# A decoder kernel on one core: every fourth product with B made by GpSimd instead of VectorE

## The chip, the cores and the metric

The kernel runs on one core of a Trainium2 chip. What counts is the device time of one execution, in microseconds (us), the median of several. The engines are named as in the profile: PE is TensorE, DVE is VectorE, ACT is ScalarE, POOL is GpSimd, SP is the queue that issues most of the DMAs.

## What is computed

A decoder over an input x of 8 batches x 256 rows x 256 channels, all in float32. First comes a stack of four layers (causal linear attention with 16 heads, then a feed-forward part), then a cosine-similarity term with a context and a small gated pair of experts, then a selective state-space mixer, a cross attention, and a mixture of eight experts with a capacity. The change touches the state-space mixer only:

```
dA = exp(einsum('bld,dn->bldn', dt, A))                 # b, l=256, d=512, n=16
u  = einsum('bld,bln->bldn', x, Bc) * dt[..., None]     # the product with B
decay = clip(floor(dA * 2**15), 0, 32767) / 2**15
h[t] = decay[t] * h[t-1] + u[t]                         # along l, for each (d, n)
y  = einsum('bldn,bln->bld', h, Cc) + x * D
```

## The kernel before

All engines run hand-written instruction streams that meet in semaphores. A batch pair (2 batches, W = 512 rows) is the unit of the outer loops; there are four pairs, p = 0 to 3. In the mixer stage the channels d lie on the partitions in four blocks of 128 (c = 0 to 3), and the 16 states n are taken two at a time (NG = 2), in eight groups g. That gives 32 units a pair, unit i being group g = i // 4 and channel block c = i % 4, so 128 units in all. Every unit works on tiles of 128 x 1024 float32 (2 states x 512 rows).

For unit i:

- ACT makes the decay: an exponential (line 921, two halves), a rounding to int16 steps (line 932) and the way back to float (line 937), into one of three buffers `dA`.
- `drive(i)` (lines 1538 to 1545) on DVE multiplies `dtx` (dt times x, channel block c) by the rows of B, and writes `uh[i % 3]`. Both inputs lie in SBUF. It waits for the rows of B (`rows_in`) and, from the fourth unit on, for `ysum_done` of unit i - 3, which used the same buffer.
- `unit(i)` (lines 1547 to 1563) on DVE: the scan along the rows (line 1555, in place in `uh`), a slice of the cross attention of the pair before (`cross(i - 1)`), `drive(i + 1)`, a slice of the next pair's first part (`head(i)`), and the product with the rows of C (line 1563, in place, both inputs in SBUF).
- `state_sum(i)` on PE (lines 2072 to 2077) adds the two states of the unit into a PSUM bank by a product with the identity (line 2076) and then raises `ysum_done`.

`mixer(p, q, n)` is called on each engine for the overlapped work of three pairs: the units of pair p, the cross attention of pair q = p - 1 and the first part ("head") of pair n = p + 1. The calls with units are (0, -, 1), (1, 0, 2), (2, 1, 3) and (3, 2, -). So the units of pair 0 have no cross slices beside them, and the units of pair 3 have no head slices.

Of POOL little is asked here. In the mixer it computes 1/sqrt(variance) for the layer norms by `deviations` (a 128 x 4 addition at line 580, a 128 x 4 power at line 581): three times a pair for the head, whose statistics DVE makes in units 0, 8 and 21 and whose results it wants in units 1, 9 and 22 (line 1426). At the end of a pair it sets the start columns of `dA` to zero (line 691). In the layer stack POOL adds bias rows (line 611, 128 x 512, and line 616, 128 x 1024) and copies rows (line 598).

Of the kernel before, what the change touches and what calls it, by code (L numbers as in the profile page):

```python
# [9 lines left out]
ALU = mybir.AluOpType  # L10
# [3 lines left out]
P = 128  # L14
# [5 lines left out]
TT = 4  # L20
W = TT * P
# [8 lines left out]
IC = DI // P  # L30
NG = 2
UNITS = NS // NG * IC
# [16 lines left out]
HEAD_STEPS, TAIL_STEPS, CROSS_STEPS = 45, 5, 6  # L49
ACT_STEPS = 2 * UNITS  # L50
CROSS_SLOTS = 38
ROUTED_EARLY = 36
VALUE_COPIES = (0, 1, 6, 8)
LAST_SLOTS = (9, 12, 15, 18, 21, 24, 27, 30)
# [77 lines left out]
def hold(eng, sem, value):  # L132

    eng.wait_ge(sem, value)
    eng.sem_inc(HELD[0], 1)
# [21 lines left out]
def ssm_and_cross(eng, body):  # L157

    body(None, None, 0)
    body(0, None, 1)
    with eng.Fori(0, PAIRS - 2) as r:
        body(r + 1, r, r + 2)
    body(PAIRS - 1, PAIRS - 2, None)
    body(None, PAIRS - 1, None)


def begun(p, q):  # L170


    if p is not None:
        return p + 1, p, 0 if q is None else q
    return (0, 0, 0) if q is None else (PAIRS, PAIRS, q)
# [27 lines left out]
def decoder(nc, t, out):  # L203
    ctx = ExitStack()

    def sem(name):
        return ctx.enter_context(nc.semaphore(name))
# [82 lines left out]
    zs, xs, dt, dtx = a(IC, W), a(IC, W), a(IC, W), a(IC, W)  # L290
# [5 lines left out]
    Bs, Cs = zip(*((a(NG, W), a(NG, W)) for _ in range(2)))  # L296
    units_at = a.at
    dA, uh = [a(NG, W) for _ in range(2)], [a(NG, W) for _ in range(2)]
# [55 lines left out]
    def cross_banks(p, n):  # L354
# [40 lines left out]
    rows_in, starts_ready = [sem(f"rows_in{j}") for j in range(2)], sem("starts_ready")  # L395
    da_ready, scan_done, hc_ready, ysum_done, yg_ready, proj_done = (
        sem(n) for n in ("da_ready", "scan_done", "hc_ready", "ysum_done", "yg_ready", "proj_done"))
    s2_done, nm_ready, pexp_ready = (sem(n) for n in ("s2_done", "nm_ready", "pexp_ready"))
    pT_done, pT_out, av2_done, at2_ready, wo2_done = (sem(n) for n in ("pT_done", "pT_out", "av2_done", "at2_ready", "wo2_done"))
    route_done, wo2_out = sem("route_done"), sem("wo2_out")  # L400
    u_ready, dtx_ready = sem("u_ready"), sem("dtx_ready")
    at2T_done, at2T_out = sem("at2T_done"), sem("at2T_out")
    xr_ready = sem("xr_ready")
    soft_e_ready, soft_u_ready, abs_ready, relu_ready = sem("soft_e_ready"), sem("soft_u_ready"), sem("abs_ready"), sem("relu_ready")
# [15 lines left out]
    GROUPS = PAIRS + 4 * L * PAIRS + PAIRS  # L420
# [153 lines left out]
    def _(pool):  # L574
        step = Steps(pool, pool_step)

        def deviations(n, c, k):

            hold(pool, var_ready, n)
            step.apart(nc.gpsimd.tensor_scalar(ve[:, c:c + k], mv[:, c:c + k, 1], LN_EPS, None, ALU.add))  # L580
            nc.gpsimd.tensor_tensor(rstd[:, c:c + k], ve[:, c:c + k], mhalf[:, 0:k], ALU.pow).then_inc(rstd_ready, 1)
# [72 lines left out]
        def send_rows(first, end, places):  # L654

            pool.wait_ge(zeroed, 16 * 4)
            pool.wait_ge(places_ready, places)
            pool.wait_ge(xf_kept, end // TT + 1)
            for i in range(first, end):
                if places == 1:  # L660
                    pool.wait_ge(av2_done, 16 * (PAIRS - 1) + i + 5)
                for k in range(2):
                    nc.gpsimd.indirect_dma_start(
                        out=rows_to, out_offset=bass.IndirectOffsetOnAxis(ap=into[k][:, i:i + 1], axis=0), in_=hst[:, i, :], in_offset=None,
                        bounds_check=NE * CAP - 1, oob_is_err=False).then_inc(scattered, 16)

        def mixer(p, q, n):
            heads, tails, ends = begun(p, q)
            groups = 3 * heads + tails + ends
            step.at(groups + 1)  # L670
            if p is None and n is None:
                send_rows(0, NT - TT, 1)
            if n is not None and p is not None:
                for k in range(3):
                    deviations(GROUPS + groups + k + 1, 0, TT)
            more = 3 if n is not None else 0
            if p is not None:
                deviations(GROUPS + groups + more + 1, 0, TT)
                more += 1
            if q is not None:  # L680
                deviations(GROUPS + groups + more + 1, 0, TT)
                hold(pool, xr_ready, q + 1)
                if p is None:
                    pool.sem_inc(xf_kept, 1)
                else:
                    nc.gpsimd.tensor_copy(hst[:, ts(q, TT), :], xr).then_inc(xf_kept, 1)
            if n is not None:

                hold(pool, dt_ready, 2 * n + 2)
                for one in dA:  # L690
                    nc.gpsimd.memset(one.rearrange("p n (s t) -> p (n s) t", s=2)[:, :, 0], 0.0).then_inc(starts_ready, 1)

        ssm_and_cross(pool, mixer)

        send_rows(NT - TT, NT, 2)
# [37 lines left out]
    def _(act):  # L733
# [92 lines left out]
        def mixer(p, q, n, head_alone=False):  # L826
# [166 lines left out]
            elif n is None:  # L993
                for i in range(CROSS_SLOTS):
                    cross(i)
# [95 lines left out]
    def _(dve):  # L1091
# [303 lines left out]
        def mixer(p, q, n, head_alone=False):  # L1395
# [4 lines left out]
            groups = GROUPS + 3 * heads + tails + ends  # L1400
# [137 lines left out]
            def drive(i):  # L1538

                g, c = i // IC, i % IC  # L1540
                if c == 0:
                    dve.wait_ge(rows_in[g % 2], 32 * (4 * p + g // 2 + 1))
                if i >= len(uh):
                    dve.wait_ge(ysum_done, UNITS * p + i - len(uh) + 1)
                v.tensor_tensor(uh[i % len(uh)], dtx[:, c, :].unsqueeze(1).broadcast_to([P, NG, W]), Bs[g % 2], ALU.mult).then_inc(u_ready, 1)  # L1545

            def unit(i):

                g, c = i // IC, i % IC
                decay, h = dA[i % len(dA)], uh[i % len(uh)]  # L1550
                flat = "p n t -> p (n t)"

                dve.wait_ge(da_ready, UNITS * p + i + 1)
                dve.wait_ge(u_ready, UNITS * p + i + 1)
                v.tensor_tensor_scan(h.rearrange(flat), decay.rearrange(flat), h.rearrange(flat), 0.0, ALU.mult, ALU.add).then_inc(scan_done, 1)  # L1555
                if q is not None and i:
                    cross(i - 1)
                if i + 1 < UNITS:
                    drive(i + 1)
                if n is not None:  # L1560
                    head(i)
                dve.wait_ge(scan_done, UNITS * p + i + 1)
                v.tensor_tensor(h, h, Cs[g % 2], ALU.mult).then_inc(hc_ready, 1)  # L1563
# [36 lines left out]
            for i in range(UNITS):  # L1600
                if p is not None:
                    unit(i)
                elif n is None and i:
                    cross(i - 1)
                    early_routing(i - 1)
# [49 lines left out]
            want += END_STEPS if first else 0  # L1655
            want += ROUTED_EARLY if p is None and n is None else 0
            assert step.n == want, (step.n, want)
# [5 lines left out]
        ssm_and_cross(dve, mixer)  # L1663
        step.at(PAIRS * (HEAD_STEPS + TAIL_STEPS + CROSS_STEPS) + END_STEPS + ROUTED_EARLY)

# [764 lines left out]
```

## Time and profile before

| | |
|---|---|
| median of 3 runs | 2406.69 us (2406.55 to 2411.33) |
| the profiled execution: its own time | 2406.48 us |
| the profiled execution: first to last instruction (span) | 2404.2 us |
| DVE busy | 1717.4 us (71%) |
| PE busy | 2071.9 us (86%) |
| ACT busy | 1045.5 us (43%) |
| POOL busy | 333.4 us (14%) |
| line 1555, scans, on DVE | 128 x 2284 ns = 292.4 us |
| line 1563, products with C, on DVE | 128 x 1218 ns = 155.9 us |
| line 1545, products with B, on DVE | 128 x 1208 ns = 154.6 us |

All times of rows are from the one profiled execution, which is 0.2 us below the median. Its 2406.48 us are the span of 2404.2 us and 2.3 us around it. In a timeline row the first number is the start in us from the start of the span, the second the duration in us. A DVE instruction's recorded duration overlaps the start of the next one by about 0.1 us, so a cost in a full queue is read from start to start.

### The profile page before, as it was taken

The page shows a single profiled execution, that of the slowest core. Times are in us where ns is not written, and L with a number is a line of the kernel's source. Part 1 is how long each engine was busy: PE and PEld are TensorE (multiplying, and loading weights), DVE is VectorE, ACT ScalarE, POOL GpSimd, SP SyncE. Part 2 cuts the span into 40 slices and gives each one's busy share as a digit, 9 for nine tenths or more (in the row PEclk, how much of TensorE's full clock was granted, in tenths as well). Part 3 has the DMA queues.
Part 4 walks back from the last instruction along what each step waited for, and adds up shares of the span by engine and source line. Part 5 has one row for each costly group of instructions (what it writes and reads, how often), then busy time and mean ns, then how long its engine had stood idle before and what let it go on. Part 6 is the DMA issues. An engine that isn't in the chain of part 4 may idle for free.

```text
span 2404.2 us, 33455 instructions
## 1 busy us (share of the span) xinstructions
PE 2071.9 (86%) x12304; PEld 1272.8 (53%) x12304; DVE 1717.4 (71%) x2514; ACT 1045.5 (43%) x1641; POOL 333.4 (14%) x368
## 2 busy tenths in 40 slices
PE   6999999999999999885659778987798888738998
PEld 4666666666666666542324344444453445525665
DVE  7777777777777778769999999989999983210001
ACT  1222222222222222328675877587758842211221
POOL 1111111111111111100000000000000001352222
PEclk8999999999999999997789888989899996669999
DMA  6000100000000100011111111111111103112442
GB/s 240 1 0 18 31 22 1 18 27 26 1 18 27 32 1 1 1 41 57 53 42 36 42 36 42 37 42 35 35 36 42 53 18 117 42 30 60 115 128 53
DMA packets 62237, 99.77 MB, mean 41 GB/s; under 512 B 13333, under 2 KB 44592, under 8 KB 61585
## 3 DMA queue, kind: packets, MB, share of 16 engines
q1 hardware_dynamic: 55120, 90.10, 11.5%
q0 software_dynamic: 6976, 7.84, 1.7%
q8 instruction: 83, 1.36, 0.2%
q14 instruction: 58, 0.47, 0.1%
HBM read 83.53 MB, written 15.53 MB: 41 GB/s over the span
## 4 chain that ended last, share of the span: by engine, by line
PE 54%; DVE 28%; issue 12%; ACT 4%; DMA 1%; another core or an unknown queue 1%; POOL 0%; DVEq 0%; SPq 0%; ACTq 0%; POOLq 0%
PE po L1806 9%; PE pa L1796 9%; DVE arena L1555 8%; PE pa L1754 4%; PE po L2347 4%; PE pa L2336 4%; DVE arena L1545 4%; PE pt L1771 4%; PE pa L2076 2%; DVE arena L1158 2%; DVE arena L1563 2%; PE pa L1786 2%; DVE arena L1160 1%; PE pa L1845 1%; PE pt L1779 1%
## 5 line engine op out<-in xcount | busy, mean ns | idle before, releaser
L2076 PE MATMUL pa<-arena 128*128 128x512 f32 x512 | 296.4, 708 | 88.2 <-DVE arena L1563 88.2
L1555 DVE TENSOR_TENSOR_SCAN arena<-arena 128x1024 f32<-128x1024 f32 x128 | 292.4, 2284 | 13.3 <-ACT arena L937 13.1
L580 POOL TENSOR_SCALAR arena<-arena 128x2 f32<-128x2 f32 (+1 forms) x92 | 27.2, 296 | 1532.1 <-DVE arena L1420 831.0
L1806 PE MATMUL po<-arena 128*128 128x256 f32 x960 | 224.2, 385 | 0.0
L2076 PEld LDWEIGHTS pa<-arena 128*128 128x128 f32 x512 | 100.2, 215 | 220.2 <-DVE arena L1563 120.0
L1796 PE MATMUL pa<-arena 128*128 128x512 f32 x480 | 212.4, 595 | 4.0 <-ACT arena L754 3.7
L776 ACT COPY arena<-pa 128x512 f32<-128x512 f32 x128 | 65.7, 601 | 323.8 <-PE pa L1754 323.8
L1233 DVE TENSOR_TENSOR arena<-pa,arena 128x512 f32<-128x512 f32 x256 | 158.6, 682 | 62.2 <-PE pa L1754 62.1
L921 ACT ACTIVATE arena<-arena 128x510 f32<-128x510 f32 x256 | 170.5, 717 | 55.1 <-DVE arena L1555 51.9
L1806 PEld LDWEIGHTS po<-arena 128*128 128x128 f32 x960 | 176.8, 189 | 32.8 <-issue 6.0
L1697 DVE TENSOR_TENSOR arena<-po,arena 128x512 f32<-128x512 f32 x14 | 9.7, 692 | 227.0 <-PE po L2347 227.0
L1545 DVE TENSOR_TENSOR arena<-arena 128x1024 f32<-128x1024 f32 x128 | 154.6, 1208 | 7.7 <-PE pa L2076 4.6
L1733 PE MATMUL po<-arena 128*128 128x128 f32 x440 | 78.6, 309 | 92.2 <-ACT arena L963 62.2
L1563 DVE TENSOR_TENSOR arena<-arena 128x1024 f32<-128x1024 f32 x128 | 155.9, 1218 | 0.3
L1796 PEld LDWEIGHTS pa<-arena 128*128 128x128 f32 x480 | 89.8, 189 | 117.2 <-issue 117.0
L932 ACT ACTIVATE arena<-arena 128x1020 int16<-128x1020 f32 x128 | 145.5, 1136 | 1.4 <-ACT arena L921 1.0
L1754 PE MATMUL pa<-arena 32*128 32x128 f32 x3072 | 128.9, 287 | 10.2 <-ACT arena L763 5.5
L937 ACT ACTIVATE arena<-arena 128x1020 f32<-128x1020 int16 x128 | 133.7, 1044 | 0.2
L1754 PEld LDWEIGHTS pa<-arena 32*128 32x128 f32 x3072 | 106.3, 189 | 50.1 <-issue 37.2
L1733 PEld LDWEIGHTS po<-arena 128*128 128x128 f32 x440 | 55.0, 159 | 142.8 <-ACT arena L963 95.4
L763 ACT ACTIVATE arena<-pa,arena 128x512 f32<-128x512 f32 x120 | 82.1, 687 | 98.4 <-PE pa L1796 98.3
L1077 ACT ACTIVATE arena<-pa,arena 128x512 f32<-128x512 f32 x64 | 43.8, 687 | 181.3 <-PE pa L2336 156.9
(255 smaller groups left out, 3779.2 us busy)
## 6 DMA issues: line engine op xcount, KB each, us to landing
arena<-bc_rows SPq DMA_DIRECT2D x64, 512.0 KB, 4.3
arena<-in_L_ffn_W SPq DMA_DIRECT2D x16, 1024.0 KB, 8.7
arena<-in_L_attn_W SPq DMA_DIRECT2D x8, 1024.0 KB, 5.7
rows_to_experts<-arena SPq DMA_DIRECT2D x4, 1024.0 KB, 13.1
arena<-rows_to_experts SPq DMA_DIRECT2D x8, 512.0 KB
out<-arena SPq DMA_DIRECT2D x5, 512.0 KB, 8.9
arena<-in_x SPq DMA_DIRECT2D x4, 512.0 KB, 7.4
arena<-in_rows SPq DMA_DIRECT2D x8, 256.0 KB, 3.2
```

Of the source, the lines that this page charges most:

```text
L921: last = a_(past_start(dA[i % len(dA)])[:, 2 * n:2 * n + 2, :], dt[:, c, :].rearrange("p (s t) -> p s t", s=2)[:, :, 1:], ACT.Exp, scale=a ...
L932: return step.mark(a_(past_start(steps16[i % 2]), past_start(dA[i % len(dA)]), ACT.Relu, scale=-DECAY_STEPS, bias=const[:, C_MID:C_MID + 1]))
L937: a_(past_start(dA[i % len(dA)]), past_start(steps16[i % 2]), ACT.Copy, scale=-1.0 / DECAY_STEPS, bias=DECAY_TOP).then_inc(da_ready, 1)
L1233: v.tensor_tensor(scm[:, (4 * block + g) % SLOTS, :, :], pa[g][:, :].rearrange("p (h q) -> p h q", h=4), tri.unsqueeze(1).broadcast_to([P, ...
L1545: v.tensor_tensor(uh[i % len(uh)], dtx[:, c, :].unsqueeze(1).broadcast_to([P, NG, W]), Bs[g % 2], ALU.mult).then_inc(u_ready, 1)
L1555: v.tensor_tensor_scan(h.rearrange(flat), decay.rearrange(flat), h.rearrange(flat), 0.0, ALU.mult, ALU.add).then_inc(scan_done, 1)
L1563: v.tensor_tensor(h, h, Cs[g % 2], ALU.mult).then_inc(hc_ready, 1)
L1733: return nc.tensor.transpose(dst, src, ident)
L1754: last = mm(pa[g][:, ts(e, P)], keys, qf[ts(g, 32), c, ts(rows_of, P)], start=True, stop=True)
L1796: last = mm(pa[(i + 2) % 4][:, :], w1[:, k, ts(i, P)], yT[:, k, :], start=k == 0, stop=k == KC - 1)
L1806: last = mm(po[s][:, ts(i, D)], gT[:, c, ts(tile, P)], w2[:, c, :], start=c == 0, stop=c == FM - 1)
L2076: last = mm(pa[c][:, :], ident, uh[i % len(uh)][:, n, :], start=g == 0 and n == 0, stop=g == NS // NG - 1 and n == NG - 1)
```

## The change

`POOL_DRIVE = 4`. The units with i % 4 == 3, those of the fourth channel block, get their product with B from POOL: 8 of 32 units a pair, 32 of 128 in all. DVE no longer issues `drive(i)` for them and waits before their scan for a new semaphore, `pool_u_ready`, in place of `u_ready`. POOL runs the same `tensor_tensor` on the same operands, after waits for `dtx`, for the rows of B and for `ysum_done` of unit i - 3. The three `deviations` of the head, which stood ahead of everything else in POOL's part of the mixer, are put between these products, after i = 0, 8 and 21.

```diff
+POOL_DRIVE = 4
...
-            if n is not None and p is not None:
-                for k in range(3):
-                    deviations(GROUPS + groups + k + 1, 0, TT)
+            def drive(i):
+
+                g, c = i // IC, i % IC
+                pool.wait_ge(dtx_ready, 2 * p + 2)
+                if i >= len(uh):
+                    pool.wait_ge(ysum_done, UNITS * p + i - len(uh) + 1)
+                pool.wait_ge(rows_in[g % 2], 32 * (4 * p + g // 2 + 1))
+                nc.gpsimd.tensor_tensor(uh[i % len(uh)], dtx[:, c, :].unsqueeze(1).broadcast_to([P, NG, W]), Bs[g % 2], ALU.mult).then_inc(pool_u_ready, 1)
+
+            if p is not None:
+                for i in range(UNITS):
+                    if i % POOL_DRIVE == POOL_DRIVE - 1:
+                        drive(i)
+                    if n is not None and i in (0, 8, 21):
+                        deviations(GROUPS + groups + (0, 8, 21).index(i) + 1, 0, TT)
...
                 dve.wait_ge(da_ready, UNITS * p + i + 1)
-                dve.wait_ge(u_ready, UNITS * p + i + 1)
+                if i % POOL_DRIVE == POOL_DRIVE - 1:
+                    dve.wait_ge(pool_u_ready, UNITS // POOL_DRIVE * p + i // POOL_DRIVE + 1)
+                else:
+                    dve.wait_ge(u_ready, (UNITS - UNITS // POOL_DRIVE) * p + i - i // POOL_DRIVE + 1)
                 v.tensor_tensor_scan(h.rearrange(flat), decay.rearrange(flat), h.rearrange(flat), 0.0, ALU.mult, ALU.add).then_inc(scan_done, 1)
                 if q is not None and i:
                     cross(i - 1)
-                if i + 1 < UNITS:
+                if i + 1 < UNITS and (i + 1) % POOL_DRIVE != POOL_DRIVE - 1:
                     drive(i + 1)
```

## Rows read from the trace of the kernel before

**Rows 1.** The page, busy tenths of DVE and POOL in 40 slices of the span.
```profile
DVE  7777777777777778769999999989999983210001
POOL 1111111111111111100000000000000001352222
```
**Rows 2.** Windows of unit loops 0, 1, 3: stretch, length; PE, PEld, DVE, ACT, POOL busy; PEclk.
```profile
1101.00:1264.00 163.00, 99.45 (x200) 41.12 (x201) 161.21 (x164) 117.13 (x146) 11.28 (x6) 0.79 0.13 45
1313.00:1509.00 196.00, 158.44 (x520) 85.40 (x519) 181.83 (x194) 146.65 (x241) 9.25 (x6) 0.86 0.12 38
1800.00:1965.00 165.00, 138.97 (x469) 70.63 (x468) 156.72 (x123) 133.16 (x223) 0.00 (x0) 0.95 0.12 41
```
**Rows 3.** Waits of DVE, 1100 to 1965: us in total, times, longest us.
```profile
DVE arena L1536 <- PE pt L2201: 13.6, 6, 3.9
DVE arena L1555 <- ACT arena L937: 13.1, 6, 5.5
```
**Rows 4.** Timeline of DVE, units 5 and 6 of pair 0: start us, us, engine, line.
```profile
1131.95 2.28 DVE L1555 TENSOR_TENSOR_SCAN arena<-arena 128x1024 f32<-128x1024 f32 x1
1134.15 1.20 DVE L1545 TENSOR_TENSOR arena<-arena 128x1024 f32<-128x1024 f32 x1
1135.26 1.22 DVE L1563 TENSOR_TENSOR arena<-arena 128x1024 f32<-128x1024 f32 x1
1136.40 2.28 DVE L1555 TENSOR_TENSOR_SCAN arena<-arena 128x1024 f32<-128x1024 f32 x1
```
**Rows 5.** POOL by line and form: count, busy us, mean ns, idle before.
```profile
L616 POOL TENSOR_TENSOR arena<-arena 128x1024 f32<-128x1024 f32 x16 | 37.9, 2367 | 0.0
```
**Rows 6.** Layer stack, POOL line 616 beside DVE line 1204; last: line 1204's durations, min/median/max.
```profile
637.12 2.36 POOL L616 TENSOR_TENSOR arena<-arena 128x1024 f32<-128x1024 f32 x1
638.43 1.60 DVE L1204 TENSOR_TENSOR_SCAN arena<-arena 128x256 f32<-128x256 f32 x1
L1204 DVE TENSOR_TENSOR_SCAN arena<-arena x64: 656/660/1607, 25.8 to 947.3; 128x256 f32<-128x256 f32 x64
```
**Rows 7.** Timelines: POOL, units 0 and 1 of pair 0 and later; DVE beside the first.
```profile
1108.16 1.00 POOL L580 TENSOR_SCALAR arena<-arena 128x4 f32<-128x4 f32 x1 [7.75 <-DVE arena L1420]
1109.34 2.76 POOL L581 TENSOR_TENSOR arena<-arena 128x4 f32<-128x4 f32 x1 [0.18 <-POOL arena L580]
...
1292.86 0.22 POOL L580 TENSOR_SCALAR arena<-arena 128x4 f32<-128x4 f32 x1 [63.52 <-DVE arena L1420]
1293.27 1.03 POOL L581 TENSOR_TENSOR arena<-arena 128x4 f32<-128x4 f32 x1 [0.18 <-POOL arena L580]
...
1107.87 1.20 DVE L1563 TENSOR_TENSOR arena<-arena 128x1024 f32<-128x1024 f32 x1
1108.98 2.29 DVE L1555 TENSOR_TENSOR_SCAN arena<-arena 128x1024 f32<-128x1024 f32 x1
1111.18 1.20 DVE L1545 TENSOR_TENSOR arena<-arena 128x1024 f32<-128x1024 f32 x1
1112.30 1.06 DVE L1426 TENSOR_SCALAR arena<-arena 128x256 f32<-128x256 f32 x3
```
**Rows 8.** A 128x1024 copy on POOL beside DVE line 1585; last: line 1585's mean of four.
```profile
1540.66 1.81 POOL L686 COPY arena<-arena 128x1024 f32 x1 [2.55 <-DVE arena L1426]
1541.61 3.01 DVE L1585 SCALAR_TENSOR_TENSOR arena<-arena 128x2048 f32<-128x2048 f32 x1
L1585 DVE SCALAR_TENSOR_TENSOR arena<-arena 128x2048 f32<-128x2048 f32 x4 | 9.9, 2472 | 0.1
```
**Rows 9.** Timelines: PE line 2076 of unit 4, pair 0, and unit 8, pair 3; DVE beside it.
```profile
1132.98 1.88 PE L2076 MATMUL pa<-arena 128*128 128x512 f32 x4
1849.35 1.99 PE L2076 MATMUL pa<-arena 128*128 128x512 f32 x4 [0.41 <-DVE arena L1563]
...
1851.41 0.66 DVE L1523 TENSOR_REDUCE arena<-pt 128x2 f32<-128x512 f32 x1
1852.82 1.22 DVE L1545 TENSOR_TENSOR arena<-arena 128x1024 f32<-128x1024 f32 x1
```

More of the change, by code:

```diff
@@ L400, in decoder @@
     route_done, wo2_out = sem("route_done"), sem("wo2_out")
-    u_ready, dtx_ready = sem("u_ready"), sem("dtx_ready")
+    u_ready, pool_u_ready, dtx_ready = sem("u_ready"), sem("pool_u_ready"), sem("dtx_ready")
     at2T_done, at2T_out = sem("at2T_done"), sem("at2T_out")
```

## The prediction

> **What bounds the kernel now.** I first read the busy tenths of the page [rows 1]: DVE stands at 9 through the slices of the mixer and POOL at 0, so there is an engine that is full beside one that is empty. The table of windows says how full [rows 2]: in the unit loop of pair 0 DVE is busy 161.2 of 163.0 us, in that of pair 1 181.8 of 196.0, in that of pair 3 156.7 of 165.0; the loop of pair 2 is like that of pair 1. ACT and PE have room in all of them. The waits of DVE over the four loops [rows 3] are few: 13.6 us for PE's output product of the cross attention (line 1536), 13.1 us for the decay (line 1555). So DVE sets the time of the units, and every microsecond put into its queue there is nearly a microsecond at the end. The timeline of one unit [rows 4] shows what it is made of: scan, product with B, product with C, 4.45 us from scan to scan (1131.95 to 1136.40) where no slice of another pair stands between.
>
> **What is removed.** DVE loses 32 products with B. In the queue one takes 1.11 us from its start to the next start (1134.15 to 1135.26), 1.12 in another place (1111.18 to 1112.30) [rows 4, 7]; the recorded 1.20 overlaps the next instruction. 32 x 1.12 = 35.8 us come off DVE.
>
> **What is added on POOL.** The nearest row is line 616, also a 128x1024 float32 product of two SBUF tensors (an addition with one operand broadcast): 2.37 us, 16 times, hardly varying [rows 5]. POOL has time for this: unit i's product may start when `state_sum(i - 3)` has ended and is due before scan i, some 7 to 9 us later in two units of 4.45 us and more. Judged by engines alone the move is free.
>
> **What it costs DVE.** It is not free, because the rows show that the two engines exclude each other. Line 616 runs from 637.12 to 639.48. DVE's line 1204, a scan with two SBUF inputs, starts at 638.43 and takes 1.60 us where its median is 0.66 [rows 6]. It ends at 640.03, so its 0.66 us of work began at 639.37: it stood still for 0.94 us and was let go 2.25 us after POOL's start. This pattern is there at 15 of the 16 executions of line 616 (the first meets an idle DVE). DVE instructions with at most one SBUF input (lines 1164 and 1197 read PSUM) run beside the same POOL work at their usual 0.74 us.
>
> The other direction is in the mixer itself [rows 7]. The 128x4 addition of line 580 starts at 1108.16 beside DVE's product with C (1107.87 to 1109.07) and ends at 1109.16, 1.00 us for a thing that takes 0.22 us undisturbed (1292.86). The power behind it, 1.03 us undisturbed (1293.27), starts at 1109.34 beside the scan of 1108.98 to 1111.27 and ends at 1112.10, 2.76 us. So a POOL instruction waits for the end of the DVE instruction that is running, has paid some 0.13 to 0.21 us of its duration by then, and gets in before the next one, although DVE's queue is full. The Trainium skill states the rule behind this (SBUF — State Buffer, "Who interferes with whom"): a VectorE instruction with two SBUF inputs and a GpSimd instruction that reads SBUF exclude each other for the whole instruction. These traces agree. The skill speaks in another place for such a move, with a caution (Perfetto Trace Analysis, "Optimizing Scalar/DVE Operations": with DVE saturated, offloading may make sense); by that alone the sum would be the first rival's below.
>
> So each of the 32 products holds DVE off for the 2.25 us less the 0.13 us already paid: 2.12 us, unless DVE has one-input work to do just then. Bounds: the whole recorded 2.36 us above. Below, the copy on POOL at 1540.66: it ends at 1542.47, and the two-input instruction that DVE started at 1541.61 took 3.01 instead of 2.47 us [rows 8], so it was held 0.54 us and let go 0.32 us ahead of the copy's end. With that early release and 0.21 us paid, the hold is 2.36 - 0.21 - 0.32 = 1.83 us. I take 2.12, since line 616 is the same kind of instruction. With no cover the change is then 32 x (2.12 - 1.12) = +32.0 us.
>
> **What covers a part of it.** Where POOL gets in depends on when `state_sum(4k)` ends. I went through all 32 hand-overs: it ends 2.04 to 5.65 us after the product with C before it. For unit 4 of pair 0 PE ends at 1134.86 [rows 9], inside the product with B that began at 1134.15 [rows 4]; POOL gets in at 1135.26, the product with C is next, and nothing covers it. For unit 8 of pair 3 PE ends at 1851.34 [rows 9], just before DVE comes to a reduction over PSUM (1851.41), a reciprocal and a product from PSUM; the next two-input instruction comes at 1852.82, so 1.41 of the 2.12 us are covered. Moving POOL's entry to the end of the two-input instruction running at the time, 15 of the 32 have no cover, and the other 17 have 11.2 us together. That leaves 32.0 - 11.2 = +20.8 us.
>
> **The small edits.** The three deviations keep their place in time, since the products 3, 7, 11, 15 and 19 are done long before the statistics that follow them. But after unit 21 the power still waits for scan 22 and ends some 0.83 us after it, as in [rows 7] (1111.27 to 1112.10); there the product with B of 1.12 us stood between scan and line 1426, and for unit 22 it is the one that is taken out. DVE will wait 0.8 us for it in pairs 0, 1 and 2: +2.4 us; no gain is possible, and without any overlap it is 1.0 us each. Product 23 is queued behind that power, and its user is scan 23, a unit later. The new waits of POOL for `dtx` and the rows of B are passed early. POOL's later work of a pair (tail deviation, copy, zeroing) comes after product 31, which is done before scan 31. SP's queue is not passed. Of DVE's waits some take up part of the delay, above all the six at line 1536 [rows 3]: a product falls between its cause and its end each time, so I take 0.5 us each, -3 us; between nothing and 6.
>
> **The sum.** -35.8 + 67.8 - 11.2 + 2.4 - 3 = +20.2 us. Against the profiled execution's own 2406.5 us that is 2426.7; it lies 0.2 us under the median, which changes nothing. I say 2426.5 us. With a hold of 1.83 us it is 9.3 us less (2417), with 2.36 us 7.7 us more (2434), and without any cover 2438.
>
> **The rivals.**
>
> First, faster: the lock costs little in the mixer, and DVE keeps its 35.8 us. For it speaks that the scan and the product next to the POOL instructions of [rows 7] have their usual durations (2.29, 1.20 us); against it that those read only 4 elements a partition, and [rows 6]. It decides below a hold of 1.12 + 0.35 (cover) = 1.47 us, which no row shows for 1024 elements. Some 5 us would go into the waits of [rows 3]: 2406.5 - 35.8 + 2.4 + 5 = 2378 us.
>
> Second, covered: once DVE is slower, PE's sums end earlier against it, so that most hand-overs of pairs 1 to 3 fall under a reduction. With every sum at 2.0 us the 32 hand-overs come to +6 instead of +20.8: 2406.5 + 6 + 2.4 - 3 = 2412 us. Against it: PE's order puts the cross attention's slices before the sum.
>
> Third, slower still: a full DVE queue keeps POOL out, and the product is only made once DVE stands waiting for it ahead of scan 4k + 3. Each then costs 2.36 plus about 0.2 us of semaphores less 1.12 = 1.44 us, 32 times +46: 2452 us. [Rows 7] speak against it.
>
> **Chances and range.** 0.60 for the forecast (its own range 2415 to 2438), 0.10 for the first rival, 0.12 for the second, 0.10 for the third, and 0.08 for mixtures of these. The range of 8 in 10 goes from the lower end of the second rival to a little above the uncovered sum: 2409 to 2442. A difference under 0.2% (4.8 us) can't be told from none here. Faster by more than that is the first rival: 0.10. Within it falls about half of the second: 0.06. Slower: 0.84.
>
> **What would show it.** In the profile after, line 1545 has 96 instructions on DVE, and POOL has 32 of about 2.4 us, longer by what they waited. DVE's two-input instructions beside them (lines 1545, 1563, 1555) have single durations that are about 2 us above the usual, 32 times less the covered ones, and the busy time of DVE in the mixer rises, although it has fewer instructions. The unit loop of pair 0 is 5 to 8 us longer than 163. DVE waits for POOL's line 581 three times more, 0.8 us each. I am wrong if no duration is stretched (first rival), if DVE waits for POOL's product ahead of every fourth scan (third), or if durations are stretched and the span doesn't follow, which would mean that PE or ACT set the loops of pairs 1 to 3.

## The result and the profile after

The changed kernel takes 2447.97 us (median of 4 runs, 2444.37 to 2455.61), the kernel before beside it 2409.01 us (4 runs); the ratio is 1.0147, with a 95% interval of 1.0116 to 1.0179. The forecast was 2426.5 us with a range of 2409 to 2442: the measured time lies above it. The sign and the mechanism of the lock are right, but the forecast has +20 us where +39 were measured. The profiled execution took 2447.95 us, its span is 2446.1 us, 41.9 us more than before.

The page of the changed kernel: busy time by engine, the tenths of DVE and POOL in 40 slices, and the groups of the mixer (line 1571 is the scan, 1579 the product with C, 1558 the product with B on DVE, 681 the one on POOL):

```profile
PE 2094.4 (86%) x12304; PEld 1285.0 (53%) x12304; DVE 1741.2 (71%) x2482; ACT 1045.5 (43%) x1641; POOL 433.0 (18%) x400
...
DVE  6777777777777788679998989898899984110101
...
POOL 1111111111111111102121111120111100343222
...
L1571 DVE TENSOR_TENSOR_SCAN arena<-arena 128x1024 f32<-128x1024 f32 x128 | 297.9, 2327 | 17.6 <-ACT arena L950 17.5
...
L1579 DVE TENSOR_TENSOR arena<-arena 128x1024 f32<-128x1024 f32 x128 | 183.5, 1434 | 1.2
L681 POOL TENSOR_TENSOR arena<-arena 128x1024 f32<-128x1024 f32 x32 | 98.5, 3078 | 445.1 <-PE pa L2092 370.4
...
L1558 DVE TENSOR_TENSOR arena<-arena 128x1024 f32<-128x1024 f32 x96 | 125.5, 1308 | 6.6 <-PE pa L2092 3.5
```

DVE has 32 instructions fewer and is busy 23.8 us longer. The mean product with C went from 1218 to 1434 ns; POOL's product is recorded with 3078 ns, 0.7 us more than the 2.37 us of its undisturbed like [rows 5].

The stretching is seen singly in the timeline. First POOL, then DVE, in units 7 and 8 of pair 0 and (second part) in unit 1:

```profile
1138.23 4.57 POOL L681 TENSOR_TENSOR arena<-arena 128x1024 f32<-128x1024 f32 x1 [21.73 <-issue]
...
1138.38 2.28 DVE L1571 TENSOR_TENSOR_SCAN arena<-arena 128x1024 f32<-128x1024 f32 x1
1140.70 3.19 DVE L1579 TENSOR_TENSOR arena<-arena 128x1024 f32<-128x1024 f32 x1
1143.81 2.28 DVE L1571 TENSOR_TENSOR_SCAN arena<-arena 128x1024 f32<-128x1024 f32 x1
...
1113.99 2.52 POOL L681 TENSOR_TENSOR arena<-arena 128x1024 f32<-128x1024 f32 x1 [0.95 <-PE pa L2092]
...
1113.24 3.42 DVE L1439 TENSOR_SCALAR arena<-arena 128x256 f32<-128x256 f32 x4
```

POOL asks at 1138.23, beside a product with C that still runs, and then stays behind the scan, whose end is at 1140.66; it runs until 1142.80. The next product with C ends at 1143.89, so its own 1.22 us began at 1142.67: DVE stood still 2.01 us from the scan's end. In the second part the four subtractions of line 1439, 1.4 us together elsewhere, take 3.42 us: one of them is held for 2 us, though it reads only one tensor from SBUF (its other operands are one value per partition).

POOL doesn't always get in behind the DVE instruction that runs when it asks. In 27 of the 32 hand-overs it does. In the other five, units 7 of all pairs and 27 of pair 0, one or two later DVE instructions go ahead of it; the longest case, POOL first, then DVE:

```profile
1250.23 6.63 POOL L681 TENSOR_TENSOR arena<-arena 128x1024 f32<-128x1024 f32 x1 [13.35 <-PE pa L2092]
...
1250.16 1.20 DVE L1558 TENSOR_TENSOR arena<-arena 128x1024 f32<-128x1024 f32 x1
1251.28 1.22 DVE L1579 TENSOR_TENSOR arena<-arena 128x1024 f32<-128x1024 f32 x1
1252.41 2.28 DVE L1571 TENSOR_TENSOR_SCAN arena<-arena 128x1024 f32<-128x1024 f32 x1
1254.73 3.21 DVE L1579 TENSOR_TENSOR arena<-arena 128x1024 f32<-128x1024 f32 x1
```

The hold on DVE is the same length then (3.21 instead of 1.22 us); it only comes later. What decides between the two orders isn't shown.

The stretches of the trace from the first to the last scan of a pair, 0 and 1 (columns as in [rows 2]), and DVE's waits over the four loops (as [rows 3]):

```profile
1103.64:1276.83 173.19, 107.24 (x202) 43.21 (x202) 170.54 (x157) 115.37 (x144) 38.17 (x14) 0.76 0.12 41
1323.65:1525.59 201.94, 155.76 (x500) 83.45 (x499) 182.11 (x180) 143.56 (x233) 34.88 (x14) 0.85 0.11 36
```
```profile
DVE arena L1549 <- PE pt L2217: 19.4, 8, 3.8
DVE arena L1571 <- ACT arena L950: 17.5, 8, 5.5
DVE arena L1439 <- POOL arena L582: 6.1, 6, 1.7
```

Against [rows 3] DVE waits 5.8 us more for PE's output product (line 1549 is the old 1536) and 4.4 us more for the decay; for POOL's power six times in all.

**How the experiments are compared.** The same kernel's time, the one before, moved between 2387.9 and 2420.5 us over the runs. In the profiles of the experiments the part behind the last scan is up to 17 us shorter than in the profile of before. So an expectation that names a time in us may be met or missed because of the part outside the loops, and differences from the kernel before that ran beside it count. Beside each ratio stand the four unit loops alone, from the first scan of a pair to its last. Between starts of DVE's instructions the time is either the slot of an instruction (start to next start) or a wait (nothing runs); summed over the loops, as differences from the profile of before:

| kernel | loops, us | of it slots | of it waits |
|---|---|---|---|
| changed kernel | +8.3 +12.0 +11.2 +9.0 = +40.5 | +24.6 | +15.9 |
| before, once more | +0.0 +0.4 +1.4 +1.2 = +3.0 | +0.4 | +2.6 |
| products left out | -6.3 +1.0 +4.4 -4.3 = -5.2 | -31.6 | +26.4 |
| memsets in their place | -2.8 +1.2 -0.7 -4.8 = -7.1 | -23.9 | +16.8 |
| delay ahead of C | +6.0 +6.2 +6.2 +4.1 = +22.5 | +25.2 | -2.8 |
| delay behind C | +6.0 +4.8 +5.2 +4.3 = +20.3 | +25.2 | -5.0 |
| both make the product | +17.6 +14.5 +21.7 +17.1 = +70.9 | +33.7 | +37.1 |
| every 8th unit | +4.7 +5.5 +8.6 +4.8 = +23.6 | +10.5 | +13.0 |
| residual later | +0.0 -0.9 +6.1 +5.7 = +10.9 | +0.9 | +10.0 |
| hold alone | +12.2 +11.3 +12.7 +10.1 = +46.3 | +47.7 | -1.4 |
| half sums | -0.0 -1.9 -1.7 +3.4 = -0.2 | -0.1 | -0.1 |
| half sums, products left out | -6.9 -7.3 -7.3 -3.7 = -25.2 | -32.5 | +7.2 |

The second row says how far the loops repeat: about 3 us in sum. It is one repetition, and every row is one profiled execution.

### The profile page after: what moved, and what is told of

Same layout as the page of the kernel before. It is cut to its first block, busy times and chain, and to the rows that moved or that the text cites. A ratio compares the mean times of both kernels' runs of the same rounds, so it can differ in the third digit from the quotient of the medians.

```text
span 2446.1 us, 33505 instructions
## 1 busy us (share of the span) xinstructions
PE 2094.4 (86%) x12304; PEld 1285.0 (53%) x12304; DVE 1741.2 (71%) x2482; ACT 1045.5 (43%) x1641; POOL 433.0 (18%) x400
## 3 DMA queue, kind: packets, MB, share of 16 engines
q1 hardware_dynamic: 55120, 90.10, 11.3%
## 4 chain that ended last, share of the span: by engine, by line
PE 52%; DVE 30%; issue 10%; ACT 4%; POOL 1%; DMA 1%; another core or an unknown queue 1%; DVEq 0%; ACTq 0%; SPq 0%; POOLq 0%
PE po L1822 9%; PE pa L1812 9%; DVE arena L1571 7%; PE pa L1770 4%; PE po L2363 4%; PE pa L2352 4%; DVE arena L1558 3%; PE pt L1787 3%; DVE arena L1579 3%; PE pa L2092 2%; DVE arena L1171 2%; PE po L2131 2%; PE pa L1802 1%; DVE arena L1173 1%; PE po L1749 1%
## 5 line engine op out<-in xcount | busy, mean ns | idle before, releaser
L2092 PE MATMUL pa<-arena 128*128 128x512 f32 x512 | 311.0, 739 | 105.1 <-DVE arena L1579 105.1
L1571 DVE TENSOR_TENSOR_SCAN arena<-arena 128x1024 f32<-128x1024 f32 x128 | 297.9, 2327 | 17.6 <-ACT arena L950 17.5
L2092 PEld LDWEIGHTS pa<-arena 128*128 128x128 f32 x512 | 105.9, 227 | 242.1 <-DVE arena L1579 137.8
L1812 PE MATMUL pa<-arena 128*128 128x512 f32 x480 | 212.5, 595 | 4.4 <-ACT arena L767 4.1
L1579 DVE TENSOR_TENSOR arena<-arena 128x1024 f32<-128x1024 f32 x128 | 183.5, 1434 | 1.2
L681 POOL TENSOR_TENSOR arena<-arena 128x1024 f32<-128x1024 f32 x32 | 98.5, 3078 | 445.1 <-PE pa L2092 370.4
L1812 PEld LDWEIGHTS pa<-arena 128*128 128x128 f32 x480 | 89.8, 189 | 118.0 <-issue 117.8
L776 ACT ACTIVATE arena<-pa,arena 128x512 f32<-128x512 f32 x120 | 82.1, 687 | 97.8 <-PE pa L1812 97.7
## 6 DMA issues: line engine op xcount, KB each, us to landing
rows_to_experts<-arena SPq DMA_DIRECT2D x4, 1024.0 KB, 13.1
```

The costliest lines, as they stand in the source:

```text
L1812: last = mm(pa[(i + 2) % 4][:, :], w1[:, k, ts(i, P)], yT[:, k, :], start=k == 0, stop=k == KC - 1)
L2092: last = mm(pa[c][:, :], ident, uh[i % len(uh)][:, n, :], start=g == 0 and n == 0, stop=g == NS // NG - 1 and n == NG - 1)
```

## The experiments

**Is it the lock?** Two kernels keep DVE's 96 products and take away POOL's reading. In the first nobody makes the product:

```diff
             if p is not None:
                 for i in range(UNITS):
-                    if i % POOL_DRIVE == POOL_DRIVE - 1:
-                        drive(i)
...
-                    dve.wait_ge(pool_u_ready, UNITS // POOL_DRIVE * p + i // POOL_DRIVE + 1)
+                    dve.wait_ge(ysum_done, UNITS * p + i - len(uh) + 1)
```

> The products with B of the 32 fourth-block units are left out altogether (their scans run over what the buffer holds), so nothing is added to POOL and DVE has only lost 32 instructions. Theory A, the two engines exclude each other and DVE sets the loops: the removal alone is worth 32 x 1.0 us (1.12 from start to start, less 0.12 us for the semaphore between scan and product with C that it had covered) = 32 us on DVE, of which longer waits for PE and ACT in the loops of pairs 1 to 3 give some back: 2375 to 2388 us. Rival B, PE or ACT set the loops of pairs 1 to 3: only the loop of pair 0 gets shorter, by 8 us: 2396 to 2404 us.

Measured: 2386.4 us beside 2397.3 us for the kernel before, ratio 0.9952 (0.9931 to 0.9972). That 2386.4 lies in the range of A is luck, since the kernel before ran 12 us faster beside it than beside the changed kernel. The loops are 5.2 us shorter: -6.3 and -4.3 us in those of pairs 0 and 3, and +1.0 and +4.4 us, so nothing gained, in those of pairs 1 and 2. DVE did lose its 31.6 us, and 26.4 us of waits took their place. Neither theory had this for all loops: A's 32 us are there as slots and not as time, and pair 3 gained against B. DVE's waits over the loops:

```profile
DVE arena L1569 <- ACT arena L948: 22.8, 13, 5.4
DVE arena L1547 <- PE pt L2215: 19.4, 9, 4.3
DVE arena L1556 <- PE pa L2090: 7.2, 3, 2.9
```

Set beside [rows 3] (13.1 us and 13.6 us in the same places), DVE waits oftener for the decay of line 948.

In the second, POOL keeps all its waits and semaphores but sets the buffer to zero twice:

```diff
...
-                nc.gpsimd.tensor_tensor(uh[i % len(uh)], dtx[:, c, :].unsqueeze(1).broadcast_to([P, NG, W]), Bs[g % 2], ALU.mult).then_inc(pool_u_ready, 1)
...
+                nc.gpsimd.memset(uh[i % len(uh)], 0.0).then_inc(pool_u_ready, 1)
+                hold(pool, pool_u_ready, 2 * (UNITS // POOL_DRIVE * p + i // POOL_DRIVE) + 1)
+                nc.gpsimd.memset(uh[i % len(uh)], 0.0).then_inc(pool_u_ready, 1)
...
-                    dve.wait_ge(pool_u_ready, UNITS // POOL_DRIVE * p + i // POOL_DRIVE + 1)
+                    dve.wait_ge(pool_u_ready, 2 * (UNITS // POOL_DRIVE * p + i // POOL_DRIVE + 1))
```

> As the changed kernel, with every wait and semaphore of the hand-over, but in place of its product POOL sets the buffer to zero twice (two memsets of 128x1024, together about 2 us), which reads nothing from SBUF; the product is thereby left out of the result. Theory A, POOL's reading excludes DVE's second input: no DVE instruction is stretched, and the time is that of the kernel with the products left out, 2375 to 2390 us. Rival C, the hand-over itself costs (DVE waits for POOL, PE's sum is late): the time is near that of the changed kernel, 2440 to 2450 us, with waits of DVE for POOL before every fourth scan.

Measured: 2381.7 us, ratio 0.9933 (0.9910 to 0.9956), the loops -7.1 us. The same hand-over without a read costs nothing: rival C falls. DVE's scans and products with C by form, then the subtractions behind the first norm beside POOL's two memsets:

```profile
L1573 DVE TENSOR_TENSOR_SCAN arena<-arena 128x1024 f32<-128x1024 f32 x128 | 292.3, 2284 | 17.5 <-ACT arena L952 17.3
...
L1581 DVE TENSOR_TENSOR arena<-arena 128x1024 f32<-128x1024 f32 x128 | 155.9, 1218 | 1.2
...
1115.57 0.95 POOL L681 MEMSET arena<- 128x1024 f32 x1 [0.95 <-PE pa L2094]
1116.68 0.95 POOL L683 MEMSET arena<- 128x1024 f32 x1 [0.15 <-POOL arena L681]
...
1114.82 2.95 DVE L1441 TENSOR_SCALAR arena<-arena 128x256 f32<-128x256 f32 x4
```

The means are to the nanosecond those of before (2284, 1218). Between this kernel and the changed one lie 47.6 us in the loops, and what POOL does in the hand-over: two writes of 0.95 us in place of one product of 2.36 us that also reads.

**Why did DVE's waits grow?** My first answer was that a hold ahead of the product with C delays PE's sum and what stands behind it. The test is the kernel before, with a reduction of 128x704 put on DVE in every fourth unit, ahead of C and, in the next one, behind it:

```diff
+    spare = ctx.enter_context(nc.sbuf_tensor("spare", [P, 8], F32))
...
+                if i % 4 == 2:
+                    v.tensor_reduce(spare[:, 0:2], dtx[:, 0:2, 0:352], AX, ALU.max)
                 dve.wait_ge(scan_done, UNITS * p + i + 1)
                 v.tensor_tensor(h, h, Cs[g % 2], ALU.mult).then_inc(hc_ready, 1)
```

> The kernel before, with one more instruction on DVE in units 2, 6, 10, ... just ahead of the product with C: a reduction of 128x704 from SBUF, about 0.78 us, 32 times, one input, so that no lock plays a part. It puts about as much time into DVE's queue as the change did net (+24.6 us from start to start). Theory A1, a delay ahead of C reaches PE's sum and the cross attention behind it, and comes back as longer waits of DVE for PE and ACT: +33 to +42 us, 2440 to 2450 us, DVE's waits in the four loops longer by 8 us or more. Rival, as predicted: the waits take up a part of the delay: +18 to +25 us, 2425 to 2432 us. Rival D, what comes on top is special to POOL (lock or semaphores): +25 us and waits unchanged.

> The same added reduction, 32 times, but just behind the product with C of units 2, 6, 10, ..., so that PE's sum of that unit isn't delayed. Theory A1 (the place matters: a hold ahead of C delays PE): +25 us, 2430 to 2434 us, and less growth of DVE's waits for PE than with the delay ahead of C. Rival (only the length of the delay matters): the same time as with the delay ahead of C, within 3 us.

Measured: 2421.8 us, ratio 1.0098 (1.0062 to 1.0134), and 2414.7 us, ratio 1.0062 (1.0036 to 1.0089). The loops say +22.5 and +20.3 us for 25.2 us of slots. So A1 falls: a delay put on DVE passes on by eight or nine parts in ten, the waits shrink a little, as the prediction had it, and the place matters by some 2 us in the loops, which is within what repeats. (The two times are 7.1 us apart, but their intervals overlap, and in the profiles the part behind the last scan is 8.7 us shorter in the second.)

**Is the removal worth anything?** Then the growth had to come with the removal and not with the hold. First try: POOL makes its product and DVE makes all 128.

```diff
                     dve.wait_ge(ysum_done, UNITS * p + i - len(uh) + 1)
+                if i % POOL_DRIVE == POOL_DRIVE - 1:
+                    dve.wait_ge(pool_u_ready, UNITS // POOL_DRIVE * p + i // POOL_DRIVE + 1)
                 v.tensor_tensor(uh[i % len(uh)], dtx[:, c, :].unsqueeze(1).broadcast_to([P, NG, W]), Bs[g % 2], ALU.mult).then_inc(u_ready, 1)
...
-                if i + 1 < UNITS and (i + 1) % POOL_DRIVE != POOL_DRIVE - 1:
+                if i + 1 < UNITS:
                     drive(i + 1)
```

> POOL makes its 32 products as in the changed kernel, and DVE makes all 128 as before (its own product for a fourth-block unit waits for POOL's and writes the same values over it). So the holds are there and nothing is removed. Theory B1: the removed products were nearly free, since DVE's waits in the loops of pairs 1 to 3 took their place (the four loops got only 5.2 us shorter when they were left out), and the whole cost of the change is the hold. Then the four loops are 42 to 52 us longer than before and the time is 2441 to 2451 us on a chip where the kernel before takes 2397, that is no more than about 8 us above the changed kernel. Rival B2: the removed products were worth their 32 us in the changed kernel too; then this is 32 us above it: +72 us, about 2470 us.

Measured: 2467.2 us, ratio 1.0293 (1.0254 to 1.0333), the loops +70.9 us. By its number that is B2, but the experiment doesn't tell the two apart, since it has a wait of its own:

```profile
DVE arena L1560 <- POOL arena L681: 36.7, 14, 4.3
```

DVE's product, one unit earlier than a scan would want it, stood 14 times and 36.7 us behind POOL's. That is a full exposure of POOL's time and no cost of the changed kernel, which never waits for line 681.

The clean form gives POOL a buffer of its own, so that nobody waits for it ahead of a scan (DVE makes all 128 products, and waits for POOL's only ahead of the product with C of the same unit, a wait that the trace never shows); POOL's product is smaller (128x800, bfloat16 output):

```diff
+    spare = ctx.enter_context(nc.sbuf_tensor("spare", [P, 2, 400], BF16))
...
-                nc.gpsimd.tensor_tensor(uh[i % len(uh)], dtx[:, c, :].unsqueeze(1).broadcast_to([P, NG, W]), Bs[g % 2], ALU.mult).then_inc(pool_u_ready, 1)
+                nc.gpsimd.tensor_tensor(spare[:, :, :], dtx[:, c, 0:400].unsqueeze(1).broadcast_to([P, NG, 400]), Bs[g % 2][:, :, 0:400], ALU.mult).then_inc(pool_u_ready, 1)
...
```

> All 128 products stay on DVE as before, nothing waits for POOL ahead of a scan. POOL additionally makes a product of 128x800 elements of the same two tensors at the place of the changed kernel's, into a spare buffer in bfloat16; it is used for nothing. So the holds stand alone (some 1.65 us each, less cover), without removal. Theory B1, the cost of the change is its holds, and they pass on to the end nearly whole: the four loops get longer by the sum of DVE's stretched slots, 36 to 46 us, with the waits of DVE changed by less than 5 us in sum. Rival B2, the hold costs more than it stretches, since what waits on PE and ACT behind it grows too (as the waits grew by 15.9 us in the changed kernel): waits +10 us or more, loops over 52 us.

Measured: 2437.3 us beside 2391.6 us, ratio 1.0182 (1.0165 to 1.0199). The loops are +46.3 us for 47.7 us of stretched slots, the waits -1.4 us: B1, a hair above its upper end. DVE's three groups by form, all longer than before (2284, 1208, 1218):

```profile
L1569 DVE TENSOR_TENSOR_SCAN arena<-arena 128x1024 f32<-128x1024 f32 x128 | 296.3, 2315 | 14.0 <-ACT arena L951 13.8
L1559 DVE TENSOR_TENSOR arena<-arena 128x1024 f32<-128x1024 f32 x128 | 174.5, 1363 | 5.4 <-issue 2.7 <-PE pa L2092 2.4 <-DVE arena L1610 0.2
L1579 DVE TENSOR_TENSOR arena<-arena 128x1024 f32<-128x1024 f32 x128 | 167.6, 1309 | 0.7
```

A hold costs what it holds. What came only in part was the gain.

**What stands in for the removed work?** If PE is the next bound, lighten it and see. Half of PE's sums left out (the second state of each unit isn't added), once with all products and once with the 32 left out as above:

```diff
-                for n in range(NG):
-                    last = mm(pa[c][:, :], ident, uh[i % len(uh)][:, n, :], start=g == 0 and n == 0, stop=g == NS // NG - 1 and n == NG - 1)
+                last = mm(pa[c][:, :], ident, uh[i % len(uh)][:, 0, :], start=g == 0, stop=g == NS // NG - 1)
```

> The kernel before with half of PE's work for the state sums left out (only the first of a unit's two states is added up), which takes about 1 us a unit from PE. It is the base for the next one. Theory B1 (PE's round trips set parts of the loops of pairs 1 to 3): those loops get shorter by 5 to 20 us together, the loop of pair 0 stays, as DVE sets it. Rival (DVE alone sets all four): within 3 us.

> The same halved sums on PE, and the 32 products with B of the fourth block left out on DVE, as in the kernel with the products left out. Theory B1: with PE lighter the removal is worth most of its 32 us: the four loops 20 to 31 us shorter than those of the kernel with halved sums alone. Rival (the removal never was worth more, for another reason, such as ACT's decays or the semaphores): 5 to 12 us shorter, as it was with PE's full work.

Measured: 2394.5 us, ratio 1.0006 (0.9989 to 1.0023), and 2376.7 us, ratio 0.9940 (0.9921 to 0.9960). With half sums alone nothing moves (the loops -0.2 us): there the rival is right, with all its products DVE sets the loops. But on that base the removal is worth 25.0 us in the loops (-25.2 against -0.2), where it was worth 5.2 us with PE's full work. The loop of pair 1 in four kernels: before, then with products left out, then half sums, then both:

```profile
1314.32:1504.25 189.93, 154.42 (x508) 83.46 (x506) 175.99 (x189) 143.75 (x233) 9.25 (x6) 0.86 0.12 38
```
```profile
1307.82:1498.77 190.95, 157.00 (x508) 85.39 (x506) 168.25 (x181) 143.63 (x233) 9.26 (x6) 0.84 0.12 38
```
```profile
1314.89:1502.96 188.07, 139.61 (x444) 78.20 (x442) 175.87 (x188) 143.80 (x233) 9.24 (x6) 0.77 0.12 38
```
```profile
1310.62:1493.28 182.66, 135.11 (x440) 75.19 (x439) 167.88 (x181) 143.62 (x233) 9.25 (x6) 0.80 0.12 39
```

DVE's busy time (third) falls by the same 8 us from 176.0 in the second and the fourth kernel; the length falls by more than 2 us only where PE's (first number) fell too. So in the loops of pairs 1 and 2 DVE and PE's path are bounds side by side: DVE is full, and right behind it stands PE. (A halved sum also hands its buffer back sooner: DVE's waits for it ahead of the product with B are 7.2 us with products left out and 1.5 us with both. These runs don't tell this from the lighter PE.)

The windows show too where the slack was small before. Length less DVE's busy time is 1.7, 13.9, 12.9 and 7.5 us in the loops of pairs 0 to 3 of the kernel before, and the removal alone gave -6.3, +1.0, +4.4 and -4.3 us there.

**Can the wait be used?** DVE waits 13.6 us ahead of the residual addition [rows 3]. The kernel before with it moved behind the product with C:

```diff
-                if q is not None and i:
+                residual = q is not None and i >= 12 and i % 8 == 4
+                if q is not None and i and not residual:
                     cross(i - 1)
...
                 v.tensor_tensor(h, h, Cs[g % 2], ALU.mult).then_inc(hc_ready, 1)
+                if residual:
+                    cross(i - 1)
```

> The kernel before with one change of order on DVE: in units 12, 20 and 28 the residual addition of the cross attention (line 1536), for which DVE waits 13.6 us in all, stands behind the product with C instead of ahead of the product with B. Theory B1 says that the loops of pairs 1 to 3 are set by the round trips between DVE, PE and ACT at such places, and not by DVE's load alone: the 2.3 us of the two products are then done inside the wait, and the three loops get 6 to 12 us shorter together, 0.3 to 0.5% of the time. Rival: DVE's load alone sets them, the wait reappears at the next slice: within 3 us.

Measured: 2401.2 us beside 2399.9 us, ratio 1.0009 (0.9986 to 1.0031), no difference, and in the profile loops that are 10.9 us longer. The wait is gone from that line and stands at the product with B:

```profile
DVE arena L1545 <- PE pa L2079: 20.3, 13, 2.9
DVE arena L1555 <- ACT arena L937: 16.8, 8, 5.5
```

My expectation of 6 to 12 us was wrong, and the move has a price of its own. PE waits for this addition before it may write the next scores (line 2085 of the kernel before, the matrix product at 2087, there 2090). PE's waits for it over the loops of pairs 1 to 3, before and here:

```profile
PE pt L2087 <- DVE arena L1536: 5.5, 7, 1.3
...
PE pt L2090 <- DVE arena L1536: 19.4, 8, 3.7
```

So the later addition made PE later by up to 13.9 us in sum, and this experiment doesn't tell whether the wait could be used if PE weren't held.

**Do the holds add up?** `POOL_DRIVE = 8` gives POOL 16 products.

> POOL makes the product of every eighth unit in place of every fourth, 16 in all. Theory: the cost is one of holds that pass through one by one, so half of the changed kernel's: the four loops +18 to +24 us against +40.5, the time +17 to +23 us. Rival: the cost comes from crowding (a hold that meets the next one's waits), and halving the number takes away more than half: under +13 us.

Measured: 2417.3 us, ratio 1.0097 (1.0059 to 1.0135), the loops +23.6 us. Half as many products and 58% of the cost in the loops, within the theory's 18 to 24 us. But the parts don't halve alike: of the slots 10.5 us remain of 24.6, of the waits 13.0 of 15.9. So the effects add up one by one roughly in the sum, and not in its parts.

A last one was the kernel before as it is.

> The kernel before, unchanged, for a profile beside the others: the stages outside the four unit loops differ between executions (the experts' stage was 7 to 16 us shorter in four of the last profiles), and the loops should be the same within 1 us each.

Measured: 2404.6 us in its one run, the loops +3.0 us together.

None of these points to a version that beats the kernel before. The three that were clearly faster (products left out, memsets, half sums with products left out) leave work out.

## Why the prediction was half right

**The lock and its length: right.** It was read from an addition in the layer stack [rows 6] and from 4-element instructions in the mixer [rows 7]. 2.12 us a product was taken; single instructions that are held whole in the timeline after are 1.97 to 2.16 us longer than usual. POOL gets in behind the running DVE instruction, as [rows 7] had shown, in 27 of 32 cases. That it is the read that locks scans and products is shown by the memsets. The rule of the Trainium skill (SBUF — State Buffer, "Who interferes with whom") says that an instruction of two SBUF inputs contends with a GpSimd instruction that reads and not with one that only writes; both halves agree with the runs.

**The cover: right in sum, in part by luck.** Holds less cover were to be 67.8 - 11.2 = 56.6 us. Measured: the slots grew by 24.6 us in the changed kernel and by -31.6 us where the products are left out, so the holds come to 56.2 us. But the prediction took DVE's work with at most one SBUF input as free of the hold. It had seen this for lines 1164 and 1197, which read PSUM. Line 1439 reads one tensor from SBUF, and seven hand-overs held it for 2.04 us each: its 56 executions take 33.5 us together in the changed kernel and 19.3 us with the products left out, so 14.2 of the 56.2 us lie there. By the prediction's rule they would have been cover.

**The removal as a slot: 4.2 us too large.** 35.8 us were counted, 31.6 came off. Some 0.12 us of each is the way from scan to product with C: the product with B starts 2.20 us after the scan's start (1131.95 to 1134.15, [rows 4]), the product with C, where it follows the scan at once, 2.32 us (1138.38 to 1140.70 above). The difference fits that C waits for the scan's semaphore and B doesn't.

**The wait for the power: right.** 2.4 us were forecast. Line 1439 waits 0.87 us in unit 22 of pairs 0, 1 and 2, +2.6 us.

**The other waits: wrong, and here is the miss.** The step was "of DVE's waits some take up part of the delay, so I take 0.5 us each, -3 us; between nothing and 6". They grew by 15.9 - 2.6 = 13.3 us, so the term was -3 where +13.3 us came. Summed: 56.2 - 31.6 + 2.6 + 13.3 = +40.5 us in the loops, and 1.4 us elsewhere make the span's 41.9. The miss of 20.3 us is this term (16.3) and the removal's slot (4.2), less 0.2 in the others. The error behind it stands in the first part: "DVE sets the time of the units, and every microsecond put into its queue there is nearly a microsecond at the end". That holds for a microsecond put in (22.5 for 25.2, 20.3 for 25.2, 46.3 for 47.7). It does not hold for one taken out (5.2 for 31.6). I took a sum of both, 20.8 us, as if only the net mattered, but a removal and a hold fall in different places: the removal gives slack, at the next meeting with PE and ACT some of the slack is waited away, and the hold then comes nearly in full. In the changed kernel the waits grew by less than in the one with the products left out (15.9 against 26.4 us), so the holds were covered by some 10 us of that slack and no more. The memset kernel had +16.8 us of waits, about as many as the changed kernel. How much the removal was worth beside the holds can only be estimated: 56.2 us of holds at the rate of the hold alone (46.3 for 47.7) are 54.6 us, the loops grew by 40.5, so it gave 14 us of its 31.6 there.

How slack is waited away is seen in the changed kernel in units 19 and 20 of pair 1. DVE, PE and ACT in turn, and last PE's sum of a unit at the same place in the kernel before:

```profile
1453.11 2.05 DVE L1486 SCALAR_TENSOR_TENSOR arena<-arena 128x256 f32 x4 [1.01 <-ACT arena L874]
...
1458.34 2.29 DVE L1571 TENSOR_TENSOR_SCAN arena<-arena 128x1024 f32<-128x1024 f32 x1 [1.92 <-ACT arena L950]
1464.35 0.42 DVE L1549 TENSOR_TENSOR arena<-pt,arena 128x256 f32 x1 [3.72 <-PE pt L2217]
...
1444.78 3.78 PE L2092 MATMUL pa<-arena 128*128 128x512 f32 x4 [2.95 <-DVE arena L1579]
1460.21 1.12 PE L1749 MATMUL po<-arena 128*128 128x128 f32 x4 [7.98 <-ACT arena L976]
...
1450.55 0.58 ACT L989 COPY arena<-po 128x512 f32<-128x512 f32 x1 [6.82 <-PE po L1749]
1451.15 1.28 ACT L874 ACT_TABLE_LOAD   x1
1452.45 2.19 ACT L874 ACTIVATE arena<-arena 128x512 f32<-128x512 f32 x4
1454.65 1.28 ACT L934 ACT_TABLE_LOAD   x1
...
1430.00 1.99 PE L2076 MATMUL pa<-arena 128*128 128x512 f32 x4 [0.23 <-DVE arena L1563]
```

ACT was held 6.82 us by PE, then does the experts' activations with a table load on either side, and its decay and the softmax behind it come late; DVE waits for it twice, PE waits 7.98 us for the softmax (line 976), and DVE 3.72 us for what PE makes of it. In the kernel before the first two waits of this place weren't there (its product with C at 1440.30 and scan at 1441.44 follow without a gap), the third was, with 3.93 us. With the products left out the scan's wait (1.92 us) and the third (4.28 us) are there; with the hold alone only the third is (3.31 us). So the new wait comes with the removal.

PE is late here for two reasons. It stood 2.95 us for the product with C of line 1579, and then the sum of unit 17 took 3.78 us, at a granted clock of 0.50 (1.2 GHz), where the same work took 1.99 us at 1.00 (2.4 GHz) in the kernel before. From this sum's start to the product for which ACT waits (line 1749) it is 5.13 us here (1444.78 to 1449.91) and was 2.66 us there (1430.00 to 1432.66), so the clock has some 2.5 of the 6.82 us for which ACT was held; before ACT was held 2.35 us. The row of busy shares doesn't tell this: PE is busy 154 of 190 us in the kernel before's loop of pair 1, and still it is next.

**What stays open.** Part of the growth is PE's granted clock, as in the place above; how much in all, no run separates. It isn't the whole: in the memset kernel the clock of the loops of pairs 1 and 2 was 0.87 and 0.87 (before 0.86 and 0.88), and the waits grew all the same; with the hold alone it was 0.86 and 0.85, and they didn't. Which of PE and ACT comes first in the ring isn't settled: lightening PE freed 19.8 us of the removal's 31.6 us, and lightening ACT wasn't tried.

**The rivals.** No contention: fell with the first stretched duration. Covered hand-overs: the holds are 56.2 us, as without it. A POOL that is kept out until DVE waits: it was kept out for one or two instructions more five times, but no wait for line 681 is among DVE's waits. That the time came out near that rival's 2452 us is a coincidence.

## What to carry to other kernels

In this kernel a product moved from VectorE to GpSimd took 1.0 us off VectorE and held it off for 1.8 us on average. Before moving anything, look in the trace for one VectorE duration stretched beside a GpSimd instruction, and look at each kind of VectorE instruction by itself, since here one with a single SBUF tensor was held too. When a change takes work out of an engine and puts a delay in, price the two apart: here a delay in a full queue passed on to 81 to 97%, while what was taken out was worth only the distance to the next engine's path, which a busy share below 100% did not show. The waits of the full engine were the sign: the two loops where it waited 13 to 14 us gave nothing back, the one where it waited 1.7 us gave back 6.3 of 8.

## What the runs showed of the hardware

POOL's memsets, which read nothing, leave scans and products with two SBUF inputs alone but stretch the 128x256 `tensor_scalar` of line 1441: four of them took 2.95 us beside two memsets of 0.95 us, against 1.4 us alone. The 128x800 product with bfloat16 output on POOL stretched DVE's slots by 47.7 / 32 = 1.5 us each, against 56.2 / 32 = 1.8 us for 128x1024 in float32. A product that waits for the scan's semaphore and follows it at once starts 0.12 us later than one that doesn't wait for it (2.32 against 2.20 us after the scan's start). And a POOL product that asked while DVE's queue was full got in behind the running instruction 27 times of 32; in unit 27 of pair 0 two more went ahead of it, and it took 6.63 us.
